# Expert products added to x by the next stage, and an earlier ranking of batch 5, in a hybrid attention and expert network

## The chip, the cores and the metric

The kernel runs on one core of a Trainium2 chip, as one program. The metric is the device time of one execution in microseconds (us), lower is better. TensorE (PE) multiplies matrices, VectorE (DVE), ScalarE (ACT) and GpSimd (POOL) do the element work, SyncE (SP) issues most transfers between HBM and the on-chip SBUF. PSUM holds what PE writes.

## What is computed

x is 8 batches of 512 rows with 128 features in float32. Seven layers follow one another, each adding to x:

```python
x = L0_attn_a_x                                                   # (8, 512, 128)
x = x + _L0_attn_a_ref(_layernorm(x), ...)                        # linear attention
x = x + _L0_ffn_ref(_layernorm(x), Wr, W1, W2)                    # experts, top 2 of 8
x = x + _L0_attn_b_ref(_layernorm(x), ...)                        # causal softmax attention, 16 heads
x = x + _L0_ffn_ref(_layernorm(x), Wr, W1, W2)                    # experts again
x = x + _L1_attn_a_ref(_layernorm(x), ...)                        # grouped attention: global, then local
x = x + _L1_ffn_ref(_layernorm(x), ...)                           # three quantized blocks with gelu
x = x + _L1_attn_b_ref(_layernorm(x), ...)                        # Toeplitz mixing over the rows
x = x + _L1_ffn_ref(_layernorm(x), ...)

def _L0_ffn_ref(h, Wr, W1, W2):
    g = jax.nn.softmax(h @ Wr, axis=-1)
    top2_w, top2_idx = jax.lax.top_k(g, 2)
    top2_w = top2_w / jnp.sum(top2_w, axis=-1, keepdims=True)
    hid = jax.nn.relu(jnp.einsum('bsh,ehf->bsef', h, W1))
    expert_out = jnp.einsum('bsef,efh->bseh', hid, W2)
    top2_out = jnp.take_along_axis(expert_out, top2_idx[..., None], axis=2)
    return jnp.sum(top2_out * top2_w[..., None], axis=2)
```

Each row goes to two experts of eight; what an expert stage adds to x is the sum of two products per row.

## The kernel before

**Stages.** x stays in SBUF as one tile `x` of 128 partitions, 32 row tiles (4 a batch) and 128 features. The program is a row of stages: linear attention, experts 1 (`moe1`), softmax attention (`soft`), experts 2 (`moe2`), grouped attention (`grp`), a feed-forward, the Toeplitz mixer, a feed-forward, the store. Each stage is one block of five instruction streams, written by hand in program order and tied by semaphores. At its end every engine drains (line 90), POOL clears each semaphore of the stage (`clear`, line 111), and all engines meet in a barrier (line 112). Only then does any engine start the next stage.

**Experts.** Routing runs inside the attention stage: per batch, `route.stats`, `power`, `apply`, `rank`, `aim` and so on find each row's two experts and its place in a list sorted by expert; POOL's `scatter` (line 826, eight indirect transfers a batch) writes the rows there in HBM. `experts_routed` then takes 72 steps of 128 sorted rows: SP fetches them, PE turns them and multiplies by W1, ACT applies relu, PE multiplies by W2, DVE weighs (line 1056), POOL sends the product to HBM at its row's place (line 975). `products` has two halves, one for each of the row's two experts. When all have arrived, SP reads them back in 8 transfers of 512 KB, a quarter of the rows and one half each (line 961), into the tile `moe_back`, and DVE adds them to x in eight additions of 128x1024 (lines 1063 and 1065), two for a quarter, each quarter as its two reads land. Then the stage ends. The second expert stage does the same, with the routing of batch 7 in front. Around each pair of an attention and an expert stage lies a stage of its own for the routing's semaphores, which clears them and meets in a second barrier.

**Softmax attention.** `stats(m)` (lines 2255, 2260) takes mean and variance of batch m, POOL's `power` (lines 1870, 1873) makes the reciprocal deviation, `apply(m)` (line 2267) the normed rows, PE turns and projects them, SP writes parts of 192 KB to HBM (line 1831), `rest_part` (line 2274) splits off what bf16 loses. There are 24 pieces (`PASS`) of scores a batch. For each, DVE takes the maxima (`maximum`, line 2283), which later enter the scores of the exponents; `split_maxima` prepares them for PE. The maxima of batch 0 stand alone, ahead of the first exponents (PE line 2132, ACT line 1977 into the tile `soft_pt`); from then on the loop over n runs the exponents of batch n beside the maxima of batch n + 1. POOL cuts the exponents at the diagonal (`keep`, line 1884). The routing of batch n - 2 is laid between: `rank` on PE and `aim` on DVE at piece 15, three scatters at pieces 18, 20, 22, five in the next batch's pass; after the last pass stand the last five of batch 5, then `number` (line 819) and the eight scatters of batch 6.

**Grouped attention.** DVE alone does most of the front: `stats(m)` (lines 1528, 1533), `apply(m)` (line 1541), a copy of the turned rows (line 1547), `copy_qkv` (line 1556), rotation and unit length (lines 1564 to 1598), with halves of the work on POOL (lines 1262 to 1275), and `quad` (lines 1604, 1605), for which PE waits with its turns (line 1405), then its scores (line 1427), then ACT's exponents (line 1350). Units 0 to 7 are the batches in the global attention, 8 to 15 those of the local one.

## Time and profile before

| | us |
|---|---|
| median of three runs | 1742.5 (1741.97 to 1743.51) |
| profiled execution | 1738.75 |
| span of its trace, first to last instruction | 1737.0 |
| PE busy | 1301.5 (75%) |
| DVE busy | 1043.5 (60%) |
| POOL busy | 848.7 (49%) |
| ACT busy | 803.1 (46%) |
| mean granted clock of TensorE | 0.877 |

The shares are means over stages with different limits; the chain that ended last has no line above 1%. What a change of one stage is worth is read from the timeline there. In a timeline row stand the start, the busy time, the engine, line, operation, the names of output and input, shapes and count, and in brackets how long the engine was idle before it and what ended that ("<-DVE soft_mx L2283": a DVE instruction of line 2283 that wrote soft_mx). "PEq", "SPq" and the like are the sequencers of the engines, "SPq DMA" a transfer's issue by SP. "x8" behind a name counts instructions grouped in one row.

### The profile page before, as it was taken

The page shows a single profiled execution, that of the slowest core. Times are in us where ns is not written, and L with a number is a line of the kernel's source. Part 1 is how long each engine was busy: PE and PEld are TensorE (multiplying, and loading weights), DVE is VectorE, ACT ScalarE, POOL GpSimd, SP SyncE. Part 2 cuts the span into 40 slices and gives each one's busy share as a digit, 9 for nine tenths or more (in the row PEclk, how much of TensorE's full clock was granted, in tenths as well). Part 3 has the DMA queues.
Part 4 walks back from the last instruction along what each step waited for, and adds up shares of the span by engine and source line. Part 5 has one row for each costly group of instructions (what it writes and reads, how often), then busy time and mean ns, then how long its engine had stood idle before and what let it go on. Part 6 is the DMA issues. An engine that isn't in the chain of part 4 may idle for free. (4 is left out here: it accounts for less than half of the span.)

```text
span 1737.0 us, 35414 instructions
## 1 busy us (share of the span) xinstructions
PE 1301.5 (75%) x11164; PEld 837.5 (48%) x11165; DVE 1043.5 (60%) x3050; ACT 803.1 (46%) x1366; POOL 848.7 (49%) x1265
## 2 busy tenths in 40 slices
PE   5773399917988888834998168888899976957486
PEld 3652399902333333324998123333455545734364
DVE  3674155438788878513554667666666525759765
ACT  1552033201666666721332047666655547634374
POOL 3277355513335555553555367676644305456242
PEclk9996699955999999966999569898999998978698
DMA  6111122255223333014222300000000000000001
GB/s 184 36 36 47 51 67 69 63 135 126 69 68 79 80 81 82 16 36 138 68 67 68 91 1 1 1 2 1 2 2 2 2 1 1 2 0 1 1 1 49
DMA packets 86677, 79.32 MB, mean 46 GB/s; under 512 B 11775, under 2 KB 76543, under 8 KB 86240
## 3 DMA queue, kind: packets, MB, share of 16 engines
q1 hardware_dynamic: 75858, 56.63, 12.9%
q0 software_dynamic: 8704, 17.97, 3.1%
q10 hardware_dynamic: 1980, 3.00, 0.9%
q8 instruction: 75, 1.23, 0.3%
q14 instruction: 60, 0.49, 0.1%
HBM read 46.07 MB, written 31.48 MB: 45 GB/s over the span
## 5 line engine op out<-in xcount | busy, mean ns | idle before, releaser
L1350 ACT ACTIVATE grp_pt<-ps 128x1024 f32<-128x1024 f32 (+2 forms) x320 | 245.1, 801 | 216.2 <-PE ps L1427 138.1
L2283 DVE TENSOR_REDUCE soft_mx<-ps 128x2 f32<-128x1024 f32 (+3 forms) x256 | 201.4, 820 | 50.0 <-PE ps L2099 49.1
L975 POOL DMA_INDIRECT products<-moe_product,moe_rows_in x144 | 156.0, 1083 | 151.0 <-DVE moe_product L1056 142.8
L1977 ACT ACTIVATE soft_pt<-ps 128x768 f32<-128x768 f32 (+1 forms) x192 | 167.2, 883 | 89.3 <-PE ps L2132 86.3
L995 ACT ACTIVATE moe_hid<-ps 128x512 f32<-128x512 f32 x144 | 86.2, 599 | 250.8 <-PE ps L1018 240.8
L1884 POOL TENSOR_SCALAR_AFFINE_SELECT soft_pt<-soft_pt 128x256 f32<-128x256 f32 (+1 forms) x192 | 93.0, 487 | 166.2 <-ACT soft_pt L1977 165.6
L1447 PE MATMUL ps<-grp_pt,grp_vpad 128*32 128x160 f32 (+4 forms) x2048 | 146.5, 395 | 16.0 <-POOL grp_pt L1292 16.0
L1018 PE MATMUL ps<-moe_rT,moe_W_now 128*128 128x128 f32 x1152 | 157.0, 280 | 1.1 <-issue 1.1
L826 POOL DMA_INDIRECT sorted_rows<-route_row,route_target x128 | 128.3, 1002 | 44.2 <-issue 31.2
L1018 PEld LDWEIGHTS ps<-moe_rT,moe_W_now 128*128 128x128 f32 x1152 | 143.5, 196 | 4.0 <-issue 4.0
L1292 POOL TENSOR_SCALAR_AFFINE_SELECT grp_pt<-grp_pt 128x256 f32<-128x256 f32 (+1 forms) x192 | 103.3, 546 | 73.8 <-ACT grp_pt L1350 73.0
L1427 PE MATMUL ps<-grp_qst,grp_kst 32*128 32x160 f16 (+4 forms) x1024 | 96.5, 279 | 8.0 <-ACT grp_pt L1350 5.6
L2151 PE MATMUL ps<-soft_pt,soft_vpad 128*32 128x512 f32 (+3 forms) x1024 | 90.3, 448 | 6.1 <-DVE route_placed L807 2.7
L1056 DVE TENSOR_SCALAR moe_product<-ps,moe_rows_in 128x128 f32<-128x128 f32 x144 | 50.5, 351 | 73.7 <-PE ps L1027 71.7
L2094 PE MATMUL ps<-soft_kst,soft_qst 64*128 64x512 bf16 (+3 forms) x512 | 72.1, 320 | 14.2 <-ACT soft_pt L1977 5.2
L1447 PEld LDWEIGHTS ps<-grp_pt,grp_vpad 128*32 128x32 f32 x2048 | 51.7, 112 | 61.7 <-POOL grp_pt L1292 24.7
L1011 PE MATMUL ps<-pack,moe_rows_in 128*128 128x128 f32 x144 | 40.5, 281 | 51.1 <-DMA moe_rows_in<-sorted_rows 51.1
L1427 PEld LDWEIGHTS ps<-grp_qst,grp_kst 32*128 32x128 f16 x1024 | 34.1, 93 | 91.2 <-ACT grp_pt L1350 46.6
L1027 PE MATMUL ps<-route_W,moe_hid 128*128 x576 | 77.9, 279 | 0.1
L1027 PE MATMUL ps<-moe_W,moe_hid 128*128 x576 | 77.0, 277 | 0.0
L1027 PEld LDWEIGHTS ps<-route_W,moe_hid 128*128 128x128 f32 x576 | 70.9, 194 | 1.2 <-issue 1.1
L1027 PEld LDWEIGHTS ps<-moe_W,moe_hid 128*128 128x128 f32 x576 | 70.2, 192 | 0.7 <-issue 0.2
(356 smaller groups left out, 2825.7 us busy)
## 6 DMA issues: line engine op xcount, KB each, us to landing
moe_rows_in<-sorted_rows SPq DMA_DIRECT2D x144, 65.0 KB, 1.8
moe_back<-products SPq DMA_DIRECT2D x16, 512.0 KB, 7.2
soft_kst<-soft_scratch_k SPq DMA_DIRECT2D x32, 192.0 KB
soft_scratch_q<-soft_parts SPq DMA_DIRECT2D x16, 192.0 KB, 2.8
soft_qst<-soft_scratch_q SPq DMA_DIRECT2D x32, 96.0 KB
soft_scratch_k<-soft_parts SPq DMA_DIRECT2D x14, 192.0 KB, 2.8
products<-moe_product,moe_rows_in POOLq DMA_INDIRECT x144
x<-in_x SPq DMA_DIRECT2D x4, 512.0 KB, 6.9
```

The costliest lines, as they stand in the source:

```text
L826: pool.indirect_dma_start(self.k.sorted_rows, bass.IndirectOffsetOnAxis(self.target[:, m % self.depth, s, j:j + 1], 0), self.row[:, m % se ...
L975: pool.indirect_dma_start(k.products, bass.IndirectOffsetOnAxis(rows_in[:, u, DEST_COL:DEST_COL + 1].bitcast(U32), 0), product[:, u, :], N ...
L1018: ins = pe.matmul(ps_hid[u % 2][:, c * P:(c + 1) * P], W1_now[:, u % 2, c * P:(c + 1) * P], rT[:, u % 2, :], start=True, stop=True)
L1027: ins = pe.matmul(ps_out[u % 2][:, 0:P], hid[:, u % 2, c * P:(c + 1) * P], W2[:, bass.ds(e, 1), c * P:(c + 1) * P].rearrange("f a h -> f ( ...
L1292: pool.affine_select(e, e, [[0, 2 if seg < 2 else 4], [1, P]], ALU.is_ge, 0.0, 0, -1).then_inc(kept.sem, 1)
L1350: act.activation(at.pair(pt[:, s % 2, :], pair, seg)[:, :, 0:w], ring[(chunks_before(m) + c) % 2][:, :, 0:w], ACT.Exp, scale=scale).then_i ...
L1427: ins = pe.matmul(ring[now % 2][:, b, col:col + w], kst[32 * g:32 * g + 32, p, j * P:(j + 1) * P], qst[32 * g:32 * g + 32, p, s, j * P:j * ...
L1447: ins = pe.matmul(sums[half][32 * g:32 * g + 32, q:q + w], vpad[:, p, j, par, g, :], at.head(pt[:, s % 2, :], g, seg, a, w), start=(par == ...
L1884: pool.affine_select(e, e, [[0, 2 if seg < 2 else 4], [1, P]], ALU.is_ge, 0.0, 0, -1).then_inc(kept.sem, 1)
L1977: act.activation(LATENT.pair(pt[:, s % 2, :], pair, seg)[:, :, 0:w], ring[second_turn(n, c) % RING3][:, :, 0:w], ACT.Exp, scale=scale).the ...
L2151: ins = pe.matmul(sums[half][32 * g:32 * g + 32, q:q + w], vpad[:, n % 2, par, j, 4 * half + g, :], LATENT.head(pt[:, s % 2, :], g, seg, a ...
L2283: ins = dve.tensor_reduce(mx[:, tile, half, :, r], ring[first_turn(n, d) % RING3][:, :, at:at + keys], AX.X, ALU.max)
```

## The change

Five edits.

1. `experts_routed` no longer adds. SP issues 16 reads of 256 KB, one for a batch and a half, and the stage ends with them under way. DVE's eight additions of 128x1024 are gone from there. Their arrival is counted in eight semaphores that outlive the stage, `k.came_back[n]`.
2. They go to a persistent buffer, `k.arena`, that the softmax stage also uses for its exponents (its `pt`). The first exponent on ACT therefore waits until all eight batches are added.
3. The next stage adds them on DVE, `add_back(n)`, two additions of 128x512 a batch. In softmax attention: batches 0, 1 and 2 ahead of their `stats`, 3 to 7 behind the maxima of pieces 3 to 7 of batch 0; `stats(3)` moves behind piece 20. In grouped attention: each batch m < 8 inside `stats(m)`.
4. The routing's semaphores are cleared with the expert stage's own: 33 clears and one barrier at the end of an expert stage where there were 38 and two. The softmax and the grouped stage have one semaphore more each, `back_added`.
5. In the last pass of softmax attention the ranking of batch 5 is at piece 7 instead of 15, its `number` at piece 8 instead of 16, and its eight scatters stand behind the odd pieces 9 to 23 instead of pieces 18, 20, 22 and the end of the pass. The waits that protect the PSUM bank of the ranking move with it.

```diff
@@ -902,7 +902,6 @@
         product = st.sb("product", [P, RING, P], F32)
-        back = st.sb("back", [P, 4, 2, 2 * T, P], F32)
         loaded = weights.loaded if weights else st.counter("loaded")
@@ -912,8 +911,7 @@
         product_ready = st.counter("product_ready", 1, 2)
-        read_back = [st.counter(f"read_back{q}") for q in range(4)]
-        added = st.counter("added", 2)
+        st.sems += route.st.sems
         block = st.block()
@@ -955,10 +953,10 @@
             hold(sp, left.sem, left.at(STEPS - 1))
-            for q in range(4):
+            for n in range(B):
                 for s in range(2):
-                    src = k.products[s * NT * P:(s + 1) * NT * P, :].rearrange("(q j p) f -> q p j f", p=P, j=2 * T)[q]
-                    sp.dma_start(back[:, q, s, :, :], src).then_inc(read_back[q].sem, 16)
+                    src = k.products[(s * B + n) * S:(s * B + n + 1) * S, :].rearrange("(j p) f -> p j f", p=P)
+                    sp.dma_start(k.back[:, n, s, :, :], src).then_inc(k.came_back[n], 16)
 
@@ -1056,13 +1054,6 @@
             ahead(dve, [(2, copy_rows), (2, copy_W1), (0, weigh)])
-
-            for q in range(4):
-                dve.wait_ge(read_back[q].sem, 32)
-                x = k.x[:, 2 * T * q:2 * T * (q + 1), :]
-                dve.tensor_tensor(x, back[:, q, 0, :, :], x, ALU.add).then_inc(added.sem, 1)
-                dve.wait_ge(added.sem, added.at(q, 1))
-                dve.tensor_tensor(x, back[:, q, 1, :, :], x, ALU.add).then_inc(added.sem, 1)
 
@@ -1176,6 +1167,7 @@
         added = st.counter("added")
+        back_added = st.counter("back_added", 2)
         block = st.block()
@@ -1517,8 +1509,18 @@
         def _(dve):
+            def add_back(n):
+                dve.wait_ge(k.came_back[n], 2 * 32)
+                x = flat(of(k.x, n))
+                dve.tensor_tensor(x, flat(k.back[:, n, 0, :, :]), x, ALU.add).then_inc(back_added.sem, 1)
+                dve.wait_ge(back_added.sem, back_added.at(n, 1))
+                dve.tensor_tensor(x, flat(k.back[:, n, 1, :, :]), x, ALU.add).then_inc(back_added.sem, 1)
+
             def stats(m):
                 p = m % 2
+                if m < B:
+                    add_back(m)
+                    dve.wait_ge(back_added.sem, back_added.at(m))
                 if m >= B:
@@ -1742,7 +1744,7 @@
         vpad = st.sb("vpad", [P, 2, 2, T, 8, 32], F32)
-        pt = st.sb("pt", [P, 2, PT], F32)
+        pt = k.arena.rearrange("p (s c) -> p s c", s=2)
         mx = st.sb("mx", [P, T, 2, 2, 4], F32)
@@ -1789,7 +1791,14 @@
         added = st.counter("added")
+        back_added = st.counter("back_added", 2)
         block = st.block()
+
+        def flat_x(n):
+            return k.x[:, n * T:(n + 1) * T, :].rearrange("p a b -> p (a b)")
+
+        def back_of(n, s):
+            return k.back[:, n, s, :, :].rearrange("p a b -> p (a b)")
 
@@ -1905,10 +1914,12 @@
                         route.scatter(pool, n - 3, 3 + c // 2)
-                    if n > 1 and c == 16:
+                    if n > 1 and c == (16 if n + 1 < B else 8):
                         route.number(pool, n - 2)
-                    if n > 1 and c in (18, 20, 22):
+                    if 1 < n < B - 1 and c in (18, 20, 22):
                         route.scatter(pool, n - 2, (c - 18) // 2)
+                    if n == B - 1 and c > 8 and c % 2 == 1:
+                        route.scatter(pool, n - 2, (c - 9) // 2)
                     if n > 0 and c == 20:
@@ -1917,8 +1928,6 @@
                         power(n + 4)
-            for i in range(3, 2 * T):
-                route.scatter(pool, B - 3, i)
             route.number(pool, B - 2)
@@ -1973,6 +1982,8 @@
                     need(act, pv_done, pv_done.at(n, s - 1))
+                if n == c == 0:
+                    act.wait_ge(back_added.sem, back_added.at(B - 1))
                 act.wait_ge(weighed.sem, weighed.at(n, c + 1))
@@ -2145,7 +2156,7 @@
                             pe.wait_ge(aT_ready.sem, aT_ready.at(n - 1))
-                        if half == 1 and n > 1:
+                        if half == 1 and 1 < n < B - 1:
                             pe.wait_ge(route.steps.sem, route.steps.at(n - 2, route.PLACED))
@@ -2167,6 +2178,8 @@
                     pe.wait_ge(rest_ready.sem, rest_ready.at(n + 3))
+                elif n == B - 2:
+                    pe.wait_ge(route.steps.sem, route.steps.at(n - 1, route.PLACED))
                 for j in range(T):
@@ -2196,11 +2209,11 @@
                 for c in range(PASS):
-                    if c == 15 and n > 1:
-                        if n + 1 < B:
-                            pe.wait_ge(m_copied.sem, m_copied.at(n + 1, 1))
-                        else:
-                            pe.wait_ge(aT_ready.sem, aT_ready.at(n - 1))
+                    if c == 15 and 1 < n < B - 1:
+                        pe.wait_ge(m_copied.sem, m_copied.at(n + 1, 1))
+                        route.rank(pe, n - 2, bank[HALF_A])
+                    if c == 7 and n == B - 1:
+                        pe.wait_ge(drained.sem, drained.at(n - 1))
                         route.rank(pe, n - 2, bank[HALF_A])
@@ -2248,9 +2261,17 @@
         def _(dve):
+            def add_back(n):
+                dve.wait_ge(k.came_back[n], 32)
+                x = flat_x(n)
+                dve.tensor_tensor(x, back_of(n, 0), x, ALU.add).then_inc(back_added.sem, 1)
+                dve.wait_ge(back_added.sem, back_added.at(n, 1))
+                dve.tensor_tensor(x, back_of(n, 1), x, ALU.add).then_inc(back_added.sem, 1)
+
             def stats(m):
...
                 need(dve, powered, powered.at(m - 2))
+                dve.wait_ge(back_added.sem, back_added.at(m))
                 for j in range(T):
@@ -2311,19 +2332,25 @@
 
+            add_back(0)
             stats(0)
+            add_back(1)
             stats(1)
...
             rest_part(0, 1)
+            add_back(2)
             stats(2)
...
             apply(2)
-            stats(3)
             for d in range(PASS):
                 maximum(0, d)
+                if 3 <= d < 3 + B - 3:
+                    add_back(d)
+                if d == 20:
+                    stats(3)
                 if d == 13:
@@ -2352,7 +2379,7 @@
                             route.gates(dve, n - 2)
-                        if c == 15:
+                        if c == (15 if n + 1 < B else 7):
                             route.aim(dve, n - 2, bank[HALF_A])
@@ -2774,6 +2801,9 @@
     k.batches_scattered = [0, 0, 0]
+    k.came_back = [ctx.enter_context(nc.semaphore(f"came_back{n}")) for n in range(B)]
+    k.arena = sb("arena", [P, 2 * PT], F32)[:, :]
+    k.back = k.arena[:, 0:B * 2 * T * P].rearrange("p (n s j f) -> p n s j f", n=B, s=2, j=T)
     k.products_sent = [ctx.enter_context(nc.semaphore(f"products_sent{u}")) for u in range(RING)]
@@ -3038,7 +3068,6 @@
         with Stage(nc, "route1") as st:
-            st.ctx.callback(st.clear)
             route = Routing(st, k, 3, IDLE)
@@ -3048,7 +3077,6 @@
         with Stage(nc, "route2") as st:
-            st.ctx.callback(st.clear)
             route = Routing(st, k, 2, 0)
```

Where DVE's adds stand is shown by its instructions in a row. `x` is the row tile, `moe_back` and `arena` hold the products, `soft_entry` is the normed batch, `soft_rest` what bf16 loses, `soft_mx` the maxima. DVE in the front of the softmax stage, before (from apply(0) and apply(1) to the first maxima):

```order
L2267 TENSOR_SCALAR soft_entry<-x,soft_mv,soft_rstd 128x128 x8
L2274 TENSOR_TENSOR soft_rest<-ps,soft_parts 128x512 x2
L2255 BN_STATS soft_bn<-x 128x6 x4
L2260 BN_AGGR soft_mv<-soft_bn 128x2 x4
L2274 TENSOR_TENSOR soft_rest<-ps,soft_parts 128x512 x2
L2267 TENSOR_SCALAR soft_entry<-x,soft_mv,soft_rstd 128x128 x4
L2255 BN_STATS soft_bn<-x 128x6 x4
L2260 BN_AGGR soft_mv<-soft_bn 128x2 x4
L2283 TENSOR_REDUCE soft_mx<-ps 128x2 x18
```

and after, up to the first adds between the maxima:

```order
L2288 TENSOR_SCALAR soft_entry<-x,soft_mv,soft_rstd 128x128 x8
L2295 TENSOR_TENSOR soft_rest<-ps,soft_parts 128x512 x2
L2267 TENSOR_TENSOR x<-arena,x 128x512
L2269 TENSOR_TENSOR x<-arena,x 128x512
L2276 BN_STATS soft_bn<-x 128x6 x4
L2281 BN_AGGR soft_mv<-soft_bn 128x2 x4
L2295 TENSOR_TENSOR soft_rest<-ps,soft_parts 128x512 x2
L2288 TENSOR_SCALAR soft_entry<-x,soft_mv,soft_rstd 128x128 x4
L2304 TENSOR_REDUCE soft_mx<-ps 128x2 x5
L2267 TENSOR_TENSOR x<-arena,x 128x512
L2269 TENSOR_TENSOR x<-arena,x 128x512
L2304 TENSOR_REDUCE soft_mx<-ps 128x2
```

Two additions stand ahead of the stats of batch 2 (and of batches 0 and 1, above these rows), and the maxima of batch 0 are broken up by the additions of batches 3 to 7; the fourth batch's stats are no longer ahead of them.

DVE in the front of the grouped stage, before, from the stats of unit 1 (`grp_bn` and `grp_mv` are the stats, `grp_h` the normed rows, `grp_qkv` the projected rows):

```order
L1528 BN_STATS grp_bn<-x 128x6 x4
L1533 BN_AGGR grp_mv<-grp_bn 128x2 x4
L1541 TENSOR_SCALAR grp_h<-x,grp_mv,grp_rstd 128x128 x4
L1547 COPY grp_xT<-ps 128x512
L1541 TENSOR_SCALAR grp_h<-x,grp_mv,grp_rstd 128x128 x4
L1528 BN_STATS grp_bn<-x 128x6 x4
L1533 BN_AGGR grp_mv<-grp_bn 128x2 x4
L1556 TENSOR_SCALAR grp_qkv<-ps,grp_factor 128x192 x4
```

and after:

```order
L1515 TENSOR_TENSOR x<-arena,x 128x512
L1517 TENSOR_TENSOR x<-arena,x 128x512
L1530 BN_STATS grp_bn<-x 128x6 x4
L1535 BN_AGGR grp_mv<-grp_bn 128x2 x4
L1543 TENSOR_SCALAR grp_h<-x,grp_mv,grp_rstd 128x128 x4
L1549 COPY grp_xT<-ps 128x512
L1543 TENSOR_SCALAR grp_h<-x,grp_mv,grp_rstd 128x128 x4
L1515 TENSOR_TENSOR x<-arena,x 128x512
L1517 TENSOR_TENSOR x<-arena,x 128x512
L1530 BN_STATS grp_bn<-x 128x6 x4
L1535 BN_AGGR grp_mv<-grp_bn 128x2 x4
L1558 TENSOR_SCALAR grp_qkv<-ps,grp_factor 128x192 x4
```

The stats of units 1 and 2 (and 0, above) have two additions ahead of them, the last pair shown standing between apply(1) and copy_qkv(0).

POOL at the end of the softmax stage's last pass, before (`route_tmp` to `route_shift` is the power of batch 6, the `L826` rows are scatters, the `L1884` rows the cuts at the diagonal, the `L819` rows a batch's `number`):

```order
L826 DMA sorted_rows<-route_row,route_target 34816x130
L712 TENSOR_SCALAR route_tmp<-route_mv 128x4
L714 TENSOR_TENSOR route_rstd<-route_tmp,route_minus_half 128x4
L716 TENSOR_SCALAR route_tmp<-route_mv 128x4
L718 TENSOR_TENSOR route_shift<-route_tmp,route_rstd 128x4
L1884 AFFINE_SELECT soft_pt<-soft_pt 128x2x128
L1884 AFFINE_SELECT soft_pt<-soft_pt 128x4x128
L826 DMA sorted_rows<-route_row,route_target 34816x130
L1884 AFFINE_SELECT soft_pt<-soft_pt 128x4x128
L826 DMA sorted_rows<-route_row,route_target 34816x130 x5
L819 CAST route_row<-pack 128x8
L826 DMA sorted_rows<-route_row,route_target 34816x130 x8
```

and after:

```order
L826 DMA sorted_rows<-route_row,route_target 34816x130
L1893 AFFINE_SELECT arena<-arena 128x2x128
L712 TENSOR_SCALAR route_tmp<-route_mv 128x4
L714 TENSOR_TENSOR route_rstd<-route_tmp,route_minus_half 128x4
L716 TENSOR_SCALAR route_tmp<-route_mv 128x4
L718 TENSOR_TENSOR route_shift<-route_tmp,route_rstd 128x4
L1893 AFFINE_SELECT arena<-arena 128x2x128
L826 DMA sorted_rows<-route_row,route_target 34816x130
L1893 AFFINE_SELECT arena<-arena 128x4x128 x2
L826 DMA sorted_rows<-route_row,route_target 34816x130
L819 CAST route_row<-pack 128x8
L826 DMA sorted_rows<-route_row,route_target 34816x130 x8
```

The five scatters of batch 5 that stood together ahead of the last `number` are among the cuts now; those of batch 6 are still the last.

## Rows read from the trace of the kernel before

**Rows 1.** Timeline, end of the first expert stage (start us, busy us, engine, ...).

```profile
347.76 11.12 SPq L961 DMA_DIRECT2D moe_back<-products  x8
...
364.43 1.23 DVE L1063 TENSOR_TENSOR x<-moe_back,x 128x1024 f32<-128x1024 f32 x1 [1.02 <-DMA moe_back<-products]
365.69 1.22 DVE L1065 TENSOR_TENSOR x<-moe_back,x 128x1024 f32<-128x1024 f32 x1
...
370.72 0.96 DVE L2255 BATCH_NORM_STATS2 soft_bn<-x 128x6 f32<-128x128 f32 x4 [3.81 <-PEq L112]
```

**Rows 2.** Line 90, that exit (duration ns min/median/max, first to last start).

```profile
L90 POOLq DRAIN  x1: 5939/5939/5939, 347.8 to 347.8; - x1
L90 SPq DRAIN  x1: 123/123/123, 358.9 to 358.9; - x1
L90 DVEq DRAIN  x1: 1264/1264/1264, 365.7 to 365.7; - x1
```

**Rows 3.** Line 111, clears at that exit and at the softmax stage's.

```profile
L111 POOLq EVENT_SEMAPHORE_RANGE_CLEAR  x38: 44/44/48, 367.2 to 370.3; - x38
...
L111 POOLq EVENT_SEMAPHORE_RANGE_CLEAR  x44: 44/44/44, 774.6 to 777.9; - x44
```

**Rows 4.** Line 90, exit of the second expert stage.

```profile
L90 SPq DRAIN  x1: 123/123/123, 963.7 to 963.7; - x1
L90 DVEq DRAIN  x1: 1261/1261/1261, 970.3 to 970.3; - x1
```

**Rows 5.** Timeline, first maxima on DVE and first exponent scores on PE.

```profile
402.40 12.89 DVE L2283 TENSOR_REDUCE soft_mx<-ps 128x2 f32<-128x1024 f32 x17
...
424.97 0.61 PE L2132 MATMUL ps<-soft_qst,soft_kst 64*128 64x512 bf16 x2 [0.18 <-DVE soft_mx L2283]
```

**Rows 6.** Stretches: window, length, busy us (count) PE, PEld, DVE, ACT, POOL; clock, DMA, GB/s.

```profile
398.00:423.00 25.00, 20.41 (x108) 5.76 (x106) 24.86 (x43) 1.25 (x3) 6.51 (x12) 0.50 0.80 168
423.00:464.00 41.00, 37.45 (x322) 13.34 (x320) 33.64 (x62) 25.73 (x35) 14.86 (x28) 0.88 0.25 63
```

**Rows 7.** Timeline, weight loads of 256 KB on SP, second expert stage.

```profile
779.10 11.05 SPq L880 DMA_DIRECT2D moe_W<-in_W  x8
```

**Rows 8.** Timeline, front of the softmax stage.

```profile
373.67 1.12 DVE L2267 TENSOR_SCALAR soft_entry<-x,soft_mv,soft_rstd 128x128 f32<-128x128 f32 x4 [0.26 <-POOL soft_rstd L1873]
...
379.39 0.69 DVE L2274 TENSOR_TENSOR soft_rest<-ps,soft_parts 128x512 f32<-128x512 f32 x1 [3.01 <-ACT soft_parts L1936]
...
382.84 1.36 SPq L1831 DMA_DIRECT2D soft_scratch_q<-soft_parts  x2
...
391.46 0.69 DVE L2274 TENSOR_TENSOR soft_rest<-ps,soft_parts 128x512 f32<-128x512 f32 x1 [8.49 <-ACT soft_parts L1936]
```

**Rows 9.** Timeline, end of the softmax stage: batch 6's routing.

```profile
745.87 1.65 ACT L724 ACTIVATE route_row<-x,route_shift,route_rstd 128x128 f32<-128x128 f32 x4 [2.14 <-POOL route_shift L718]
...
759.89 0.98 POOL L826 DMA_INDIRECT sorted_rows<-route_row,route_target  x1 [3.88 <-DVE route_target L814]
```

**Rows 10.** Timeline, front of the grouped stage.

```profile
979.34 1.11 DVE L1541 TENSOR_SCALAR grp_h<-x,grp_mv,grp_rstd 128x128 f32<-128x128 f32 x4 [1.38 <-POOL grp_rstd L1237]
...
982.95 1.12 DVE L1541 TENSOR_SCALAR grp_h<-x,grp_mv,grp_rstd 128x128 f32<-128x128 f32 x4 [0.54 <-POOL grp_rstd L1237]
...
985.43 1.39 DVE L1556 TENSOR_SCALAR grp_qkv<-ps,grp_factor 128x192 f32<-128x192 f32 x4 [0.16 <-PE ps L1390]
986.86 0.49 DVE L1564 TENSOR_TENSOR grp_prod<-grp_qkv,pack 128x320 f32<-128x320 f32 x1
986.90 1.24 POOL L1262 TENSOR_TENSOR grp_prod<-grp_qkv,pack 128x320 f32<-128x320 f32 x1 [1.88 <-DVE grp_qkv L1556]
...
987.27 1.23 DVE L1565 TENSOR_TENSOR grp_prod<-grp_qkv,pack 128x320 f32<-128x320 f32 x1
...
1016.19 1.35 DVE L1604 TENSOR_TENSOR grp_quad<-grp_unit,grp_quad 128x1024 f16<-128x1024 f32 x1 [1.75 <-POOL grp_quad L1275]
```

**Rows 11.** Timeline, first pass of the grouped loop.

```profile
1042.60 1.74 DVE L1604 TENSOR_TENSOR grp_quad<-grp_unit,grp_quad 128x1024 f16<-128x1024 f32 x1 [1.66 <-POOL grp_quad L1275]
```

## The prediction, on record before the changed kernel was run

> **What bounds the kernel now.** I read the profiled execution (span 1737.0 us, its run 1738.75 us; the three runs have a median of 1742.5, so 3.75 is added at the end) in this order: the table of stretches for who is busy, the timeline at the two exits of the expert stages for who comes last, the rows of line 90 and line 111 for what an exit consists of, and then, for each place where an add is put, the DVE row behind it and what that row waited for. One core, no engine bounds the whole: each stage is a chain, and the edits touch three of them.
>
> At the end of the first expert stage SP starts the eight reads at 347.76, and they hold it for 11.12 us [rows 1]. DVE adds quarter by quarter; the last quarter's first add starts at 364.43, having waited 1.02 us for the reads, and the last one at 365.69 [rows 1]. The drains say who is last: POOL's ends at 347.8 + 5.9 = 353.7, SP's at 358.9 + 0.12 = 359.0, DVE's at 365.7 + 1.26 = 367.0 [rows 2]. From there 38 clears run until 370.3 [rows 3] and the soft stage's first DVE instruction starts at 370.72 [rows 1]. So the exit waits for the adds alone, 8.0 us behind the next one, SP. The second expert stage repeats it: SP done at 963.8, DVE at 971.6 [rows 4], 7.8 us.
>
> In the soft stage the first maxima stand between the projections and the first exponents: 17 of them run without a gap in 12.89 us, and the first exponent scores on PE start only at 424.97, 0.18 us after the maxima they wait for [rows 5]. In the table of stretches DVE is busy 24.86 of 25 us there, PE 20.41 at a clock of 0.50, which is the lower of its two levels, 1.2 GHz [rows 6]. From 423 to 464 PE is the fuller engine, 37.45 of 41 us, and DVE has 7.4 us idle [rows 6]: work put ahead of 425 is paid in full, work behind it may be free.
>
> **The two exits.** Removed: DVE's eight adds from the path. The last engine is then SP, if its 16 reads of 256 KB take no longer than eight of 512 KB. Nearest rows: eight weight loads of 256 KB, behind one of 2 MB, hold SP 11.05 us for the same 4 MB in all [rows 7]; two unhindered issues of 192 KB take 1.36 us, 0.68 each [rows 8], so 16 of them 10.9. Both give 11 us, so I take zero, with up to +0.5 each. Then come the clears. Two groups of callbacks (38 clears, two barriers) become one of 33 with one barrier. The exit of the soft stage, 44 clears and one barrier, takes 3.3 us for 44, 0.077 each [rows 3]; five fewer are 0.4, and a barrier less I put at 0.2. The first exit gains 8.0 + 0.6 = 8.6, the second 7.8 + 0.6 = 8.4, **17.0 us in all**, ends 15.5 and 17.0.
>
> **What an add costs.** A batch needs two additions of 128x512. The row of that shape is 0.69 us [rows 8]; the step between two adds today is 365.69 - 364.43 = 1.26 for 1.23 of work [rows 1], 0.03 for the wait. So a batch is 2 x 0.72 = 1.44 us; eight cost 11.5 on DVE per expert stage where before they cost 9.8. What matters is where they stand.
>
> **Front of the soft stage.** Batches 0 and 1 stand ahead of apply(0), which today waits 0.26 us for POOL's power [rows 8]: 2 x 1.44 less that wait = +2.6. Each of the two is needed before its stats, so neither can slide. Batch 2 stands ahead of stats(2), and DVE then idles 8.49 us before the next rest part [rows 8]: hidden. Batches 3 to 7 stand between the first maxima, in DVE's gapless stretch, ahead of the exponents: 5 x 1.44 = 7.2, or 6.5 if the fixed part of an add (2 x 0.69 - 1.23 = 0.15 us) is hidden by its neighbour each time; I take **7.0**. stats(3) goes from ahead of maximum 0 to behind maximum 20, still ahead of the exponents: nothing is won, and +0.1 is for its wait. Sum of the first transition: -8.6 + 2.6 + 7.0 + 0.1 = **+1.1 us**. It costs as much as it frees.
>
> **End of the soft stage.** The rank of batch 5 moves from c = 15 to c = 7 and its eight scatters are issued between the keeps of the last pass instead of behind it. That would pay if POOL's scatters of batch 6 waited for POOL. They don't: the first starts at 759.89 after 3.88 us in which it waited for DVE's targets [rows 9]. The targets come from batch 6's routing, and that starts with ACT's rows, which waited 2.14 us for POOL's shift [rows 9]; POOL now issues more scatters, about 1 us each, in front of that shift. Bounds 0 and +0.8; I take +0.3. The added clear is another 0.08. **+0.4.**
>
> **Front of the grouped stage.** The adds of batches 0 and 1 stand ahead of apply(0), which today starts at 979.34 after 1.38 us of waiting for POOL [rows 10]: 2 x 1.44 - 1.38 = +1.5. apply(1) takes 0.5 of that back from its own wait of 0.54 us for POOL [rows 10] (+1.0 there); the add of batch 2 puts 1.44 more ahead of copy_qkv(0), whose slack is its 0.16 us wait for PE [rows 10]: +2.4 less 0.16, so +2.3 there, all told. The add of batch 3 stands in DVE's row of work that ends in the quads of unit 1; POOL waits for DVE, DVE 1.75 us for POOL [rows 10], and PE, then ACT, for those: a chain, so +1.4. Batches 4 to 7 come in the loop, where DVE waits 1.66 us for POOL's quads right behind the stats [rows 11]: 1.44 fits, and the next waits are no shorter. **Sum: -8.4 + 2.3 + 1.4 = -4.7 us.**
>
> **What POOL and DVE do to each other.** The same product of 128x320 takes 0.49 us at 986.86 and 1.23 at 987.27, where POOL runs its own product of two SBUF tiles beside it [rows 10]. The new adds, two SBUF inputs each, meet POOL's power instructions at three places (batch 1 in either front, batch 2 in the grouped one). Where they meet, one waits for the other, up to 0.74 each, so 0 to +2.2 in all; half the meetings would be met by idle time. I take +0.8. The Trainium skill, "SBUF — State Buffer", section "Who interferes with whom", says that a DVE instruction with two SBUF inputs contends with a GpSimd instruction that reads SBUF, and not with one that only writes. It speaks against this change, and the pair of rows above agrees with it; taken at each of the three places it would make the sum 1.4 us worse than mine.
>
> **Sum.** +1.1 + 0.4 - 4.7 + 0.8 = -2.4 on 1738.75. Two small costs are not in the trace: the new stage's code and first small transfers start while reads are still landing (the last at 364.4, and the stage would now start at 362.1), and PE's clock, which rises from 0.50 after the exponents begin, may rise a step later. Bounds 0 and +2; I take +0.4. That leaves **-2.0**: 1738.75 - 2.0 = 1736.75 for a run like the profiled one, 1742.5 - 2.0 = **1740.5** against the median.
>
> **The rivals.**
> 1. *Forecast*, small gain, -4 to +0.5: 1738.5 to 1743.0. Chance 0.50.
> 2. *The adds are partly free.* If the adds of batches 3 to 7 fall where PE, at its low clock, is the slower (it is busy 20.4 of 25 us) and the queue of full PSUM banks lets DVE catch up, some 3 us of the 7.0 go, and -2.0 becomes -5: 1737.5. Against: DVE has 0.14 us idle in that stretch [rows 6]. With the contention left out too it would be -6, 1736.5. Chance 0.18.
> 3. *More is lost in the fronts.* Contention at its bound (+1.4 more), the clock a step later (+1.5), SP held 0.5 longer twice: -2.0 + 3.9 = +1.9, 1744.4. Chance 0.17.
> 4. *The stage's end still waits for the reads.* If SP's drain (or the barrier behind it) completes only when the last read has landed, the soft stage's exit starts at 364.4 instead of 359.0, 5.4 us later, and likewise the second: -2.0 + 10.8 = +8.8, **1751.3**. This ends slower; the sum turns positive from 1 us of extra wait per exit, and passes +3.5 from 2.8. Against: today's drain on SP takes 0.12 us at 358.9 [rows 2], while reads that DVE still waits for at 364.4 are under way. Chance 0.10.
> 5. *The change doesn't do what it says*, because SP's issue goes by the number of reads: at 11.05/8 = 1.38 us each, 16 take 22 us, SP ends 11 us later than today's SP and 3 later than today's DVE. Each exit loses 3 instead of gaining 8: -2.0 + 22 = +20, 1762.5. Against: the 0.68 us of an unhindered issue. Chance 0.05.
>
> **How the numbers follow.** Likeliest is the first: 1740.5. The range takes in cases 1 to 3 with their bounds, 1736.5 to 1745.5, and leaves out cases 4 and 5 and a little of the tails, under 2 in 10. A measurement of this kernel can tell about 0.2%, 3.5 us, from no change. Faster by more than that (under 1739.0): all of case 2 but a little, and an eighth of case 1 and more, together 0.30. Slower (over 1746.0): cases 4 and 5 and a tip of case 3, 0.17. Within: 0.53.
>
> **What would show each step.** Right: SP's 16 reads take 11 to 11.5 us; SP's drain is under 0.2 us and ends last; 33 clears in 2.5 us; the soft stage's first DVE instruction 8.5 us earlier than 370.7; DVE gapless through the first maxima, and the first exponent scores near 426, 1 us later than 424.97; the soft stage's end 1 to 2 us later than it was; the grouped stage's first exponent some 4.7 us earlier, counted from the end of the expert steps. Wrong: the adds of 128x512 longer than 0.69 throughout; a gap on DVE between maxima and adds while it waits for reads; the adds of batches 4 to 7 moving ACT's row in the grouped loop; SP's drain over 1 us. If the seventeen maxima with their adds take less than 17 us, case 2 holds; if PE's clock stays at 0.50 for more than 8.5 us behind the first exponents, case 3.

## The result, and the profile after

The change makes the kernel slightly slower. Over 20 runs each, side by side, the changed kernel has a median of 1742.75 us (1735.55 to 1746.73) and the kernel before 1734.99 (1729.57 to 1744.23). The medians are 7.8 us apart; the ratio over all runs is 1.0037, 95% interval 1.0023 to 1.0051, so +6.4 us of 1735. The forecast was -2.0 us, 1740.5, with a range of 1736.5 to 1745.5. The time lies in that range by luck: the three runs of before that were shown (median 1742.5) were among its slowest. The sign is wrong. The kernel before scatters by 15 us from run to run; part of this scatter, the experiments show, sits in the loop that the change upsets.

The profiled execution after took 1744.38 us with a span of 1742.6; before it was 1738.75 and 1737.0. Walking both timelines from anchor to anchor (starts of the same instruction, us):

| stretch | before | after | change | forecast |
|---|---|---|---|---|
| last product sent to first DVE instruction of the soft stage | 25.25 | 17.42 | -7.8 | -8.6 |
| from there to the first exponent on ACT | 54.90 | 64.30 | +9.4 | +9.7 |
| to the first scatter of batch 6 | 334.27 | 332.84 | -1.4 | +0.4 |
| last product of the second expert stage to first grouped exponent | 56.40 | 50.40 | -6.0 | -4.7, contention aside |
| first to last grouped exponent | 414.4 | 425.4 | **+11.0** | 0 |

Beyond the table, +0.9 us was there before the first expert stage ended, in code that the change leaves alone, +0.8 came up in the second expert stage's steps, and the stages behind the grouped one were 1.2 shorter; together +5.6, the difference of the spans. As for the -1.4 us in the third row, run a3 below shows that the trace of before was unlucky there by 1.9.

Both exits went nearly as forecast. Timeline of the first one, after (start, busy us, engine, line, operation; in brackets idle before and what ended it), and the drains and clears there (duration min/median/max in ns, first to last start):

```profile
346.35 0.96 POOL L973 DMA_INDIRECT products<-moe_product,moe_rows_in  x1 [0.30 <-issue]
348.66 11.78 SPq L959 DMA_DIRECT2D arena<-products  x16
...
363.77 0.69 DVE L2267 TENSOR_TENSOR x<-arena,x 128x512 f32<-128x512 f32 x1 [17.80 <-PEq L112]
```

```profile
L90 POOLq DRAIN  x1: 5939/5939/5939, 348.7 to 348.7; - x1
L90 SPq DRAIN  x1: 122/122/122, 360.5 to 360.5; - x1
```

```profile
L111 POOLq EVENT_SEMAPHORE_RANGE_CLEAR  x33: 44/44/48, 360.8 to 363.4; - x33
```

SP is last, at 360.6. Its drain takes 0.12 us with reads under way (the last packets of these reads end at 363.9), and 33 clears take 2.6 us, where DVE's drain at 367.0 and 38 clears stood in [rows 2] and [rows 3]. Sixteen issues hold SP 11.78 us, 0.66 more than eight did in [rows 1].

DVE among the first maxima, after, the answer to [rows 5]:

```profile
396.98 4.13 DVE L2304 TENSOR_REDUCE soft_mx<-ps 128x2 f32<-128x1024 f32 x5
401.04 0.67 DVE L2267 TENSOR_TENSOR x<-arena,x 128x512 f32<-128x512 f32 x1
401.75 0.69 DVE L2269 TENSOR_TENSOR x<-arena,x 128x512 f32<-128x512 f32 x1
402.36 0.95 DVE L2304 TENSOR_REDUCE soft_mx<-ps 128x2 f32<-128x768 f32 x1
403.22 0.68 DVE L2267 TENSOR_TENSOR x<-arena,x 128x512 f32<-128x512 f32 x1
```

An add and its partner take 0.68 and 0.69 us, back to back with the maxima, and DVE is busy 31.73 of 32 us in the stretch from 393 to 425 (24.86 of 25 in [rows 6]). Five pairs cost 6.6 us.

The loss sits in the grouped loop. The stretch from the first to the 200th exponent of the grouped stage, ten units, in both kernels (window, length, then busy us and count of PE, weight loads, DVE, ACT, POOL, then the granted clock, DMA share, GB/s). Before:

```profile
1006.40:1257.60 251.20, 209.05 (x2043) 88.89 (x2047) 172.74 (x380) 165.12 (x202) 168.18 (x300) 0.90 0.01 1
```

after:

```profile
1002.20:1264.40 262.20, 217.29 (x2041) 96.11 (x2045) 180.85 (x390) 164.86 (x201) 170.12 (x299) 0.87 0.00 1
```

ACT does the same work in the same time. DVE has 8.1 us more, 7.3 of it ten additions: the pair of batch 3, which falls behind the first exponent, and the four pairs of batches 4 to 7. PE has 8.2 us more for the same matmuls, at a mean granted clock of 0.87 instead of 0.90.

Now the place where batches 4 to 7 are added, the first pass of the loop, after:

```profile
1037.28 0.68 DVE L1515 TENSOR_TENSOR x<-arena,x 128x512 f32<-128x512 f32 x1
1037.99 0.78 DVE L1517 TENSOR_TENSOR x<-arena,x 128x512 f32<-128x512 f32 x1
...
1040.90 1.76 DVE L1606 TENSOR_TENSOR grp_quad<-grp_unit,grp_quad 128x1024 f16<-128x1024 f32 x1 [0.81 <-POOL grp_quad L1267]
```

```profile
1037.23 2.03 POOL L1284 TENSOR_SCALAR_AFFINE_SELECT grp_pt<-grp_pt 128x256 f32<-128x256 f32 x2 [0.46 <-ACT grp_pt L1342]
1039.22 1.33 POOL L1266 CAST grp_quad<-grp_unit 128x1024 f16<-128x1024 f32 x1
```

and the same place on POOL before:

```profile
1039.61 0.41 POOL L1292 TENSOR_SCALAR_AFFINE_SELECT grp_pt<-grp_pt 128x256 f32<-128x256 f32 x1 [0.46 <-ACT grp_pt L1350]
1040.31 0.64 POOL L1292 TENSOR_SCALAR_AFFINE_SELECT grp_pt<-grp_pt 128x512 f32<-128x512 f32 x1 [0.29 <-ACT grp_pt L1350]
1040.90 1.35 POOL L1274 CAST grp_quad<-grp_unit 128x1024 f16<-128x1024 f32 x1
```

The pair of additions fits into DVE's wait as forecast: 1.66 us of idle in [rows 11], 0.81 now. But the idle should have shrunk to 0.2. It did not, because POOL is later: its two cuts at the diagonal took 0.41 and 0.64 us, 1.29 from the start of the first to the cast; beside the additions they take 2.03, and the cast comes 1.99 us behind the first cut, 0.70 later. What waits for that cast is DVE's quads, PE's turns and then the next unit's scores.

This is the first of four passes, and the only one of this trace with such a delay. In the second, third and fourth the cuts take 0.41 and 0.75 us and the cast comes 1.40 us behind the first of them, 0.11 late. The second, on POOL:

```profile
1067.05 0.41 POOL L1284 TENSOR_SCALAR_AFFINE_SELECT grp_pt<-grp_pt 128x256 f32<-128x256 f32 x1 [1.11 <-ACT grp_pt L1342]
1067.76 0.75 POOL L1284 TENSOR_SCALAR_AFFINE_SELECT grp_pt<-grp_pt 128x512 f32<-128x512 f32 x1 [0.29 <-ACT grp_pt L1342]
1068.45 1.33 POOL L1266 CAST grp_quad<-grp_unit 128x1024 f16<-128x1024 f32 x1
```

### The profile page after: what moved, and what is told of

Its sections match the earlier page's. It is cut to its first block and busy times, and to the rows that moved or that the text cites. A ratio compares the mean times of both kernels' runs of the same rounds, so it can differ in the third digit from the quotient of the medians.

```text
span 1742.6 us, 35420 instructions
## 1 busy us (share of the span) xinstructions
PE 1310.9 (75%) x11164; PEld 847.4 (49%) x11165; DVE 1050.1 (60%) x3066; ACT 802.3 (46%) x1366; POOL 850.3 (49%) x1265
## 3 DMA queue, kind: packets, MB, share of 16 engines
q8 instruction: 75, 1.23, 0.3%
## 5 line engine op out<-in xcount | busy, mean ns | idle before, releaser
L1988 ACT ACTIVATE arena<-ps 128x768 f32<-128x768 f32 (+1 forms) x192 | 167.2, 882 | 90.2 <-PE ps L2143 87.1
L1893 POOL TENSOR_SCALAR_AFFINE_SELECT arena<-arena 128x256 f32<-128x256 f32 (+1 forms) x192 | 92.9, 487 | 141.6 <-ACT arena L1988 140.8
L826 POOL DMA_INDIRECT sorted_rows<-route_row,route_target x128 | 127.1, 993 | 46.2 <-issue 29.9
L2162 PE MATMUL ps<-arena,soft_vpad 128*32 128x512 f32 (+3 forms) x1024 | 91.0, 451 | 7.1 <-POOL arena L1893 3.0
L1439 PEld LDWEIGHTS ps<-grp_pt,grp_vpad 128*32 128x32 f32 x2048 | 52.4, 114 | 64.2 <-POOL grp_pt L1284 26.1
L2143 PE MATMUL ps<-soft_qst,soft_kst 64*128 64x256 bf16 (+3 forms) x512 | 68.2, 307 | 3.4 <-DVE soft_mx L2304 3.2
```

What stands on the lines that cost most here:

```text
L826: pool.indirect_dma_start(self.k.sorted_rows, bass.IndirectOffsetOnAxis(self.target[:, m % self.depth, s, j:j + 1], 0), self.row[:, m % se ...
L1439: ins = pe.matmul(sums[half][32 * g:32 * g + 32, q:q + w], vpad[:, p, j, par, g, :], at.head(pt[:, s % 2, :], g, seg, a, w), start=(par == ...
L1893: pool.affine_select(e, e, [[0, 2 if seg < 2 else 4], [1, P]], ALU.is_ge, 0.0, 0, -1).then_inc(kept.sem, 1)
L1988: act.activation(LATENT.pair(pt[:, s % 2, :], pair, seg)[:, :, 0:w], ring[second_turn(n, c) % RING3][:, :, 0:w], ACT.Exp, scale=scale).the ...
L2162: ins = pe.matmul(sums[half][32 * g:32 * g + 32, q:q + w], vpad[:, n % 2, par, j, 4 * half + g, :], LATENT.head(pt[:, s % 2, :], g, seg, a ...
```

## Experiments

The kernels of one letter ran beside the same runs of the kernel before, on one chip; a ratio is always to those. "Loop" is the time from the first to the last grouped exponent. The theory after reading the traces: the grouped loop's adds cost the 11 us. The rival: the soft stage's part, or the earlier start, costs, and the loop's clock fell by chance.

**a1: adds only in the soft stage.** The second expert stage adds all eight batches itself, each as its two reads land; the grouped stage adds none.

```diff
+            for n in range(here):
+                dve.wait_ge(k.came_back[n], 32 * (earlier + 1))
+                x = k.x[:, n * T:(n + 1) * T, :].rearrange("p a b -> p (a b)")
+                dve.tensor_tensor(x, k.back[:, n, 0, :, :].rearrange("p a b -> p (a b)"), x, ALU.add).then_inc(added.sem, 1)
...
             def stats(m):
                 p = m % 2
-                if m < B:
-                    add_back(m)
-                    dve.wait_ge(back_added.sem, back_added.at(m))
```

The first lines stand at the end of DVE's stream in `experts_routed`, with `here` 8 in the second expert stage and 0 in the first.

> The changed kernel, but the second expert stage adds all eight batches itself, each as its two reads land, and the grouped stage adds nothing. Theory (the grouped loop is where the time goes: the trace of after has the first grouped exponent 4.2 us earlier than before and the last ones 6.8 us later): the loss goes away. Against the kernel before: the soft front and maxima +1.5 to +2.5, the earlier scatters of batch 5 -2.2, the second exit about -1.5, so -2 us, ratio 0.998 to 1.000. Rival (the first transition is what costs, the grouped loop only shows a clock that fell by chance): as slow as the changed kernel, 1.003 to 1.005.

Measured: ratio 0.9998 (0.9977 to 1.0019), median 1731.95 us. First to last grouped exponent 411.7 us.

**a2: adds only in the grouped stage.** The mirror image, and the scatters of batch 5 at their old places.

> The changed kernel, but the first expert stage adds all eight batches itself, the soft stage adds nothing, has its stats(3) in front and its scatters of batch 5 at their old places. Only the grouped stage adds. Theory (adds in the grouped loop cost more than the earlier start brings): slower than before by +3 to +7 us, ratio 1.002 to 1.004; the grouped exponents again start some 6 us early against the expert steps and end late. Rival (the soft part costs): at or below the kernel before, 0.995 to 1.000.

Measured: 1.0007 (0.9989 to 1.0026), median 1735.26; the profiled run, 1739.5 us, has a loop of 425.5. So neither part alone is clearly slower. For a2 the expected +3 us or more did not show, although its profiled loop is as slow as that of the changed kernel: its runs spread from 1728.8 to 1740.0, and the profiled one is near the top. Why its median is so low is taken up at the end.

**a3: only the earlier ranking and scatters of batch 5, in the kernel before.**

> The kernel before with only the earlier ranking and scatters of batch 5. The prediction had +0.3 us for it. The trace of after has the first scatter of batch 6 only 1.0 us later than before where the last maxima were 3.2 us later, so 2.2 us were won there. If that is the scatters' doing: -2 us, ratio 0.9985 to 0.999, and the last scatter of batch 6 ends 2 us earlier in the trace. If it came from something else: 1.000.

Measured: 1.0002 (0.9982 to 1.0023). From the last soft exponent to the first scatter of batch 6 the trace of before has 11.8 us (748.09 to 759.89), and this one 9.9. But a2, which has the old places, has 9.9 as well. The trace of before was 1.9 us unlucky there, and edit 5 is worth nothing that these runs can measure; the changed kernel and a1 have 9.5 and 9.3. The -2 us was a miss, read out of one pair of traces.

**a4: the changed kernel without the additions in the loop.** Batches 4 to 7 stay without their expert products.

> The changed kernel with the additions of batches 4 to 7 in the grouped loop left out (x of those batches lacks the expert products; all else runs). Theory (those four pairs of additions, 1.44 us each, lengthen DVE's turn in the loop and with it tip TensorE's clock): faster than the changed kernel by 5.8 us for the adds alone and up to 11 with the clock, so 1732 to 1737 where the changed kernel has 1743, ratio to before 0.996 to 0.999; the clock in the units 1 to 7 above the 0.89 it has in after. Rival (the adds are hidden as the prediction had it, and the loss is the clock's by the stage's earlier start): within 2 us of the changed kernel, ratio 1.002 to 1.004.

Measured: 0.9995 (0.9971 to 1.0018), median 1731.75, loop 414.7. The adds in the loop cost the whole loss and more: 11 us from one median to the other, and the same again between c1 and c4 below, which ran side by side.

**b1: the loop's additions in another place.** Between the copy of the turned rows and copy_qkv, where DVE waits some 2.5 us for PE.

```diff
             def stats(m):
                 p = m % 2
+                if m < 4:
+                    add_back(m)
                 if m < B:
-                    add_back(m)
...
                 copy_xT(m + 2)
+                if m + 4 < B:
+                    add_back(m + 4)
                 copy_qkv(m + 2)
```

> The changed kernel with one thing moved: the additions of batches 4 to 7 stand in the grouped loop between the copy of the turned rows and copy_qkv, where DVE sits idle 2.45 to 2.78 us waiting for PE in both traces, and not inside stats. Theory (the adds are on DVE's path between apply and the quads, 1.44 us each, and the longer turn costs clock besides): the loop, 425.4 us from first to last exponent in the changed kernel, returns to 412 to 415, and the kernel is at 1731 to 1734, ratio to before 0.997 to 1.000. Rival (any two-input work of DVE in the loop costs that much, wherever it stands, because POOL is held up): the loop stays at 423 to 425 and the ratio at 1.003.

Measured: 0.9995 (0.9971 to 1.0019), median 1732.37, loop 414.3. The same four pairs, 10 us cheaper, so the place decides.

**b2: two maxima in place of two additions.** The same place as in the changed kernel and the same time, 0.67 and 0.69 us, but one SBUF input (expert products of batches 4 to 7 left out).

```diff
+                elif m < B:
+                    dve.wait_ge(k.came_back[m], 2 * 32)
+                    dve.tensor_reduce(spare[:, 0, :], flat(of(k.x, m)), AX.X, ALU.max).then_inc(back_added.sem, 1)
+                    dve.wait_ge(back_added.sem, back_added.at(m, 1))
+                    dve.tensor_reduce(spare[:, 1, :], flat(of(k.x, m)), AX.X, ALU.max).then_inc(back_added.sem, 1)
```

> The changed kernel, but in the grouped loop the two additions of each of the batches 4 to 7 are replaced by two maxima over 128x512 with one SBUF input, about as long (left out: the expert products of those batches). Theory (DVE's time in that place is what costs): the loop takes 423 to 426 us as in the changed kernel, ratio 1.003 to 1.005. Rival (an addition reads two SBUF tiles and so stands in the way of POOL's casts and cuts): the loop falls to 416 to 420, since only DVE's own time is left, ratio 1.000 to 1.002.

Measured: 0.9974 (0.9958 to 0.9989), median 1731.43, faster than either theory had it, and yet the profiled run, at 1737.8 us the slowest of the twelve, has a loop of 422.4 us.

**b3: only batch 4 added in the loop** (5 to 7 left out).

> The changed kernel with only batch 4 added in the grouped loop, batches 5 to 7 left out. Without any of the four the loop took 414.7 us, with all four 425.4. Theory A (each pair costs 1.44 us, and the lower clock comes with the sum): a quarter, 416 to 418. Theory B (one longer turn already shifts PE's pauses so that the clock falls in every following unit): 420 to 422, 5 us of the 11 with a quarter of the work.

Measured: 0.9989 (0.9966 to 1.0011), loop 414.2. One batch does not tip it, although its pass has the 0.70 us delay in full (the cast 1.99 us behind the first cut). Theory B falls, and the quarter of theory A (416 to 418) does not show either.

The next four settle how far this repeats.

> The changed kernel once more, unaltered, beside the next three on one chip. If its loss is real and not a matter of the chip or the day: ratio to before 1.002 to 1.005, first to last grouped exponent 423 to 426 us, as the two traces with all four pairs of additions in the loop have it (425.4 and 425.5).

Measured (the changed kernel, unaltered): 1.0044 (1.0025 to 1.0062), loop 424.1.

> The kernel with maxima in place of the loop's additions, once more (left out: the expert products of batches 4 to 7). Its first trace has a slow loop, 422.4 us, in a run that was its slowest (1737.8 where the median was 1731.4). If that loop was an exception: a loop of 412 to 417 and a ratio of 0.997 to 0.999, so DVE's time in that place is not what costs. If the fast runs were the exception: a loop of 421 to 425 and a ratio above 1.001.

Measured: 0.9993 (0.9970 to 1.0015), median 1731.31, and now a loop of 411.6.

> The same with four maxima for each of the batches 4 to 7 instead of two, 2.7 us of DVE in place of 1.4 (left out: the expert products of those batches). Theory DVE time (a longer turn of DVE costs, itself and through the clock): clearly slower than with two, by 5.4 us and more, ratio above 1.001, a loop of 422 to 430. Theory second input (what costs is that the additions read two SBUF tiles beside POOL): no slower than with two but for what exceeds DVE's idle time, at most 1 us a batch, ratio below 1.000.

Measured: 1.0034 (1.0016 to 1.0052), median 1739.79, loop 422.2. So "second input" alone is not the cause either: 2.7 us of DVE with one input do nearly the same harm as 1.4 us of additions.

> The changed kernel without the loop's additions, once more, beside the others (left out: the expert products of batches 4 to 7). 1731 to 1733, ratio 0.997 to 1.000, a loop of 412 to 416; the difference to the unaltered changed kernel of the same call is the price of the four pairs: 7 to 11 us.

Measured: 0.9999 (0.9975 to 1.0022), median 1730.87; the profiled run took 1743.9 us and its loop, **without the additions of batches 4 to 7**, 425.7 us, where 412 to 416 was expected. This is the most telling run of the study. The loop can take a fast or a slow course, and the four pairs are not needed for the slow one. One unit shows it, the third (its 20 exponents), in c4:

```profile
1057.10:1084.10 27.00, 22.82 (x210) 10.03 (x210) 16.85 (x39) 16.55 (x22) 16.82 (x33) 0.87 0.00 1
```

in c2, with the maxima:

```profile
1054.40:1078.30 23.90, 19.86 (x210) 8.44 (x210) 18.12 (x42) 16.54 (x21) 16.81 (x33) 1.00 0.00 1
```

and in before and after:

```profile
1058.70:1082.60 23.90, 19.90 (x210) 8.44 (x210) 16.75 (x40) 16.56 (x21) 16.82 (x33) 1.00 0.00 1
```

```profile
1057.00:1084.10 27.10, 22.74 (x210) 9.98 (x210) 18.38 (x42) 16.54 (x21) 17.02 (x33) 0.87 0.00 1
```

The same 210 matmuls take PE 19.9 us at a granted clock of 1.00 (2.4 GHz throughout) and 22.8 at 0.87 (part of the time at 1.2 GHz), and the unit takes 3.1 us longer. With or without 1.4 us more on DVE makes no difference to either number.

Unit by unit, from first exponent to first exponent, the third to the eighth take 27.1, 26.3, 26.6, 23.5, 27.1 and 23.0 us in the changed kernel. In a2, c4 and d1 the same six agree with these within 0.2 us, whatever DVE was given to do. In the kernel before they take 23.9, 26.1, 25.4, 21.5, 26.6 and 23.3. So the slow course is a regular one, in which the clock falls in each of these units, and in the fast course it falls in some and spares others: in the trace of before two of the six have a granted clock of 1.00, in that of the changed kernel none has more than 0.92. Over the ten units:

| kernel | profiled run, us | work added per pass | ten units | clock | runs above 1739 us |
|---|---|---|---|---|---|
| before | 1738.8 | none | 251.2 | 0.90 | 4 of 35 (beside the c kernels; 23 of 142 in all) |
| a4, c4 | 1733.0, 1743.9 | none | 251.4, 262.4 | 0.90, 0.87 | 6 of 24 |
| b3 | 1729.2 | two additions in one pass alone | 250.9 | 0.90 | 1 of 12 |
| b1 | 1732.7 | pair in the idle place | 251.0 | 0.90 | 3 of 12 |
| b2, c2 | 1737.8, 1728.8 | two maxima, 1.4 us | 259.1, 248.3 | 0.87, 0.91 | 1 of 24 |
| c3 | 1740.2 | four maxima, 2.7 us | 258.9 | 0.88 | 8 of 12 |
| d1 (below) | 1739.1 | four maxima, 2.7 us | 259.9 | 0.87 | 6 of 12 |
| after, c1 | 1744.4, 1742.5 | two additions, 1.4 us | 262.2, 260.9 | 0.87, 0.87 | 28 of 32 |

The last column is a rough sign and not a count of slow loops. Most runs have no trace, the rest of the program scatters too (the trace of before, 1738.8, has a fast loop, and that of b2, 1737.8, a slow one), and the mark suits only kernels whose other stages take about as long as those of before.

c4 in the course of the changed kernel (windows over its ten units):

```profile
1001.70:1264.10 262.40, 217.96 (x2040) 95.02 (x2044) 174.70 (x382) 164.68 (x201) 168.37 (x299) 0.87 0.00 1
```

**d1: the kernel before with nothing but a longer turn of DVE**, four maxima per pass in its loop, results unused.

```diff
             def stats(m):
+                if 4 <= m < B:
+                    for i in range(4):
+                        dve.tensor_reduce(spare[:, i, :], flat(of(k.x, m)), AX.X, ALU.max)
```

> The kernel before, with four maxima over 128x512 (2.7 us of DVE, results unused) in the grouped loop ahead of the stats of each of the batches 4 to 7; nothing else is changed. Theory clock mode (the loop has a fast and a slow course, 411 to 415 and 422 to 426 us, told apart by how often TensorE's clock falls, and a longer turn of DVE drives it into the slow one): slower than before by 7 to 10 us, ratio 1.004 to 1.006, most runs above 1739, loop 420 to 426, although the kernel has neither the early start nor the adds. Rival (the slow course comes from the earlier start of the stage or from arena and the reads still landing): the ratio stays under 1.002 and the loop at 412 to 416.

Measured: 1.0034 (1.0016 to 1.0052), median 1739.02, loop 423.1. The ratio is a little under the forecast, and half of its runs, not most, lie above 1739. Its ten units:

```profile
999.30:1259.20 259.90, 216.34 (x2044) 94.85 (x2048) 181.90 (x396) 164.82 (x202) 167.64 (x300) 0.87 0.01 1
```

No earlier start, no arena, no reads in flight, and the slow course all the same. The rival falls: a longer turn of DVE in these passes is enough.

**Why additions and not maxima.** In c2 the maxima stand where the additions stood, and POOL's cuts beside them, on DVE and POOL:

```profile
1035.37 0.67 DVE L1527 TENSOR_REDUCE grp_spare<-x 128x1 f32<-128x512 f32 x1
...
1038.31 1.77 DVE L1613 TENSOR_TENSOR grp_quad<-grp_unit,grp_quad 128x1024 f16<-128x1024 f32 x1 [0.23 <-POOL grp_quad L1268]
```

```profile
1035.31 0.41 POOL L1285 TENSOR_SCALAR_AFFINE_SELECT grp_pt<-grp_pt 128x256 f32<-128x256 f32 x1 [0.46 <-ACT grp_pt L1343]
1036.02 0.64 POOL L1285 TENSOR_SCALAR_AFFINE_SELECT grp_pt<-grp_pt 128x512 f32<-128x512 f32 x1 [0.29 <-ACT grp_pt L1343]
1036.60 1.36 POOL L1267 CAST grp_quad<-grp_unit 128x1024 f16<-128x1024 f32 x1
```

0.41 and 0.64, and 1.29 us from cut to cast, as before. DVE's idle shrinks from 1.66 to 0.23, just as the prediction had it. In this first pass DVE takes, from the start of apply to the start of the quads, 4.05 us in the kernel before and 4.06 with two maxima, but 4.74 with two additions (through POOL) and 4.93 with four maxima (through DVE itself, whose idle is then gone). To the end of the quads, for which PE waits, it is 6.30, 6.34, 7.01 and 6.54: with four maxima the quads themselves are shorter, 1.30 us instead of 1.77 for the first.

So both kernels with a slow loop are later in that pass, by 0.7 and 0.2 us at the end of the quads, and the one with two maxima is not. How much delay it takes, and in how many passes, is not shown. The full delay stands in one pass of each trace with additions (the first in the changed kernel and in a2, the second in c1), and b3 with one such pass kept the fast course. In the later passes the measure fails, because a unit in which the clock falls lengthens it too: in the kernel before, with nothing added, it is 4.05, 3.98, 4.95 and 4.96 us in the four passes.

**d2: other places in the same two stages.** The changed kernel, batches 3 to 7 of the soft stage behind stats(2), stats(3) back in front, and b1's place in the loop.

```diff
             stats(2)
+            for n in range(3, B):
+                add_back(n)
...
-                if 3 <= d < 3 + B - 3:
-                    add_back(d)
-                if d == 20:
-                    stats(3)
```

> The changed kernel with its adds in other places of the same stages: batches 3 to 7 in the soft stage behind stats(2), where DVE waits 8.5 us, none between the maxima, stats(3) back in front; batches 4 to 7 in the grouped loop between the copy of the turned rows and copy_qkv. Theory: the 6.6 us between the maxima are saved in full (first exponents 6 to 7 us earlier against the last product), the loop is in its fast course in most runs: 1724 to 1728, ratio 0.993 to 0.997. Rival (adds hide nowhere in the soft front, since PE and POOL are slowed or delayed by them): 1730 to 1733.

Measured: 0.9967 (0.9945 to 0.9988), median 1726.96. The loop of the profiled run is 417.6 us, between the fast and the slow ones, and two of the twelve runs lie 8 and 11 us above the median, so a slow loop now and then is not excluded. The first exponent comes at 420.10, 75.1 us behind the last product, where the changed kernel has 81.7: the 6.6 us between the maxima come back in full.

**b4 and d3: the version that is faster than both.** Batches 0 to 3 are added inside the expert stages, under SP's issues, and 4 to 7 as in d2.

> All adds where DVE is idle: batches 0 to 3 in each expert stage itself, while SP still issues the later reads; batches 4 to 7 in the soft stage behind stats(2), in front of the 8.5 us in which DVE waits, with nothing between the first maxima and stats(3) back in front; in the grouped stage batches 4 to 7 between the copy of the turned rows and copy_qkv. Everything else as in the changed kernel. Theory (place decides): against before, first transition -8.6 to -6, second -8.4 to -6, tail -0.5, so -13 to -17 us, about 1719 to 1722, ratio 0.990 to 0.993; first maxima 8 us earlier against the last product than before. Rival (the gains at the exits are given back wherever the adds stand, by the clock): 0.998 to 1.000.

Measured: 0.9896 (0.9871 to 0.9922), median 1716.76, 18 us under the kernel before, loop 409.6. Once more:

> The kernel with batches 0 to 3 added inside the expert stages and 4 to 7 in DVE's idle places, once more for its interval: 1715 to 1719, ratio 0.988 to 0.992, no run above 1725. If its six fast-loop runs were luck, some runs lie 10 us higher.

Measured: 0.9904 (0.9880 to 0.9928), median 1718.13, loop 413.1; no run of the twelve in both is above 1721.71. The end of b4's first expert stage on DVE, and the two drains:

```profile
351.47 0.69 DVE L1062 TENSOR_TENSOR x<-arena,x 128x512 f32<-128x512 f32 x1 [6.35 <-DMA arena<-products]
...
357.53 0.69 DVE L1064 TENSOR_TENSOR x<-arena,x 128x512 f32<-128x512 f32 x1
362.48 0.87 DVE L2286 BATCH_NORM_STATS2 soft_bn<-x 128x6 f32<-128x128 f32 x4 [4.25 <-PEq L112]
```

```profile
L90 DVEq DRAIN  x1: 728/728/728, 357.5 to 357.5; - x1
L90 SPq DRAIN  x1: 122/122/122, 359.1 to 359.1; - x1
```

Four batches are added and DVE's drain is over by 358.2, before SP's ends at 359.2. They are free, and nothing stands ahead of the first stats of the next stage.

## Why the prediction was wrong

**The exits: right.** Forecast -8.6 and -8.4 with SP's drain last; the first measured -7.8. Most of the missing 0.8 us is SP, held 0.66 longer by 16 reads than by 8, a little over the +0.5 allowed for it. The second gained 8.2 (25.31 us from the last product to DVE's first instruction, now 17.14). Rivals 4 and 5 (a drain that waits for the reads, issues by number) are refuted by the 0.12 us drain and the 11.78 us.

**The price of an add: right.** 0.68 and 0.69 us, 1.40 a pair, against 1.44.

**The fronts and the maxima: right.** 9.4 us against 9.7 from the soft stage's start to its first exponent, +6.6 of it between the maxima (forecast 7.0, bounds 6.5 to 7.2). The contention forecast in the fronts (+0.8) is there, but did less: POOL's power takes 1.45 us instead of 1.04 in either front, and neither is waited for longer. The grouped front cost 2.2 us (8.2 less 6.0) where the forecast had 3.7 before contention; it was counted too high. Beside POOL's low parts (two SBUF inputs against two) the additions of batch 2 took 1.65 and 1.52 us, in a hidden place. The first:

```profile
377.12 1.65 DVE L2267 TENSOR_TENSOR x<-arena,x 128x512 f32<-128x512 f32 x1
```

**The end of the soft stage:** forecast +0.3 and 0.08; the runs of a3 show nothing of that size, and their interval of 0.2% either way could not.

**The step that failed** is the sentence on batches 4 to 7: "1.44 fits, and the next waits are no shorter". It fits on DVE: the waits in the four passes of before are 1.66, 1.59, 2.57 and 2.57 us (the second is a little shorter, against the words, and still long enough), and two maxima of the same length in the same place show that DVE's time alone would have been free (0.9974 and 0.9993). So the sum had these four pairs at nothing, and they cost the loop 11.0 us between the two traces. Two things were missing. First, the contention that I priced at three places in the fronts was not priced in the loop, where it matters: POOL's cuts stand beside these additions and read SBUF, and in the first pass the cast behind them comes 0.70 us later. The rows 0.49 against 1.23 us in [rows 10] had shown the mechanism. The Trainium skill, "SBUF — State Buffer", section "Who interferes with whom", gives the rule for it (a DVE instruction with two SBUF inputs contends with a GpSimd instruction that reads SBUF); the cuts at 0.41 and 0.64 us beside maxima, and 2.03 for the two beside additions, agree with it. Second, a delay in that loop is not paid one for one. It makes the slow course likelier, in which TensorE's granted clock is 0.87 over the ten units instead of 0.90 or 0.91, and that course costs 8 to 11 us. That work on DVE in this place brings it on is shown by c3 and d1; that the additions do so through POOL's cuts is argued from the first pass and from the maxima that did not. In the forecast, the clock had one line, "a step later", +1.5 us. Rival 3 had both words, contention and clock, in the wrong place and at a seventh of the size.

**The median compared with.** The forecast was set against 1742.5, three runs that all lay in the upper part of the kernel's own spread; the 20 runs have 1734.99. One profiled execution of a kernel that scatters by 15 us is one draw, and differences of 2 us between two traces (the 1.9 us at the end of the soft stage) can be draws too.

**The run a2.** It has the changed kernel's loop additions and a loop of 425.5 us, yet a median of 1735.26. Its other stages explain that. Against the trace of before it gains 2.9 us up to the first soft exponent (77.23 instead of 80.15 us behind the last product) and 5.8 in the second transition (50.58 instead of 56.40), and loses 11.1 in the loop: +2.4 in all, inside its interval of -1.9 to +4.5. A fast loop would put it near 1726, an estimate from the same figures, and 10 of its 12 runs are above 1731. So it does not speak against the loop's additions.

**What stays open.** What decides the course of a single run is not settled, nor how much delay tips it. And b2 and c2, with two maxima, are in the slow course less often (1 of 24 above 1739, and b2's trace besides) than a4 and c4 without them (6 of 24), which no theory here explains; with such counts it may be chance.

## What to carry to other kernels

A wait of DVE that another engine ends can take work only if that work leaves the other engine alone. An addition of two SBUF tiles beside POOL work can lengthen POOL's (2.03 us for two cuts) and so come back as the very wait it was put into, or be lengthened itself (1.65 us instead of 0.69). Before work goes into a loop whose granted clock is below full, look at that clock in several executions and not in one; here four pairs of additions that DVE had time for cost 11 us. And when transfers are left under way across a stage's end, put the consumers where their engine is idle in both stages: with four batches under the issues and four in DVE's long waits, the kernel gained 18 us, where the other places lost 6.

## What was not expected of the hardware

Two executions of one program differ by 11 us in 250 over the same work (c4: 262.4 us at a granted clock of 0.87; a4, the same code: 251.4 at 0.90). ACT's busy time there is the same within 0.2 us, and PE's is 9.6 us longer. Issuing 16 reads of 256 KB holds SP 11.78 us against 11.12 for 8 of 512 KB, so for the same 4 MB each further read costs only 0.08 us. A drain of the issuing engine takes 0.12 us while its reads are still landing, the last of them 3.3 us later (360.6 to 363.9).
